# Attention scores with two heads per 32-row group of queries and keys, in a fused AdaLN block and rotation

## The chip, the cores and the metric

One core of a Trainium2 chip runs one program. The metric is device time in microseconds, the median of several executions. A core has five engines with queues of their own: TensorE (PE, with its weight loads PEld), VectorE (DVE), ScalarE (ACT), GpSimd (POOL) and SyncE (SP), which issues the DMAs here. They meet at semaphores only. Matmuls write PSUM, eight banks of 512 f32 columns on 128 partitions.

## The reference

Everything is f32. B = 16 sequences, L = 128 tokens, C = 144 channels, H = 16 heads of D = 9.

```python
ada = silu(c) @ W_ada + b_ada
shift_msa, scale_msa, gate_msa, shift_mlp, scale_mlp, gate_mlp = split(ada, 6)
h = modulate(layernorm(x), shift_msa, scale_msa)
q, k, v = heads(h @ W_qkv + b_qkv)
attn = softmax((q * D ** -0.5) @ k.T)               # per sequence and head, 128 x 128
x = x + gate_msa * ((attn @ v) @ W_proj + b_proj)
h = modulate(layernorm(x), shift_mlp, scale_mlp)
x = x + gate_mlp * (gelu(h @ W_fc1 + b_fc1) @ W_fc2 + b_fc2)
U, _ = qr(P)                                        # P is 144 x 64
R = expm(A)                                         # A skew, 64 x 64, one for each sequence, from silu(cond) @ W.T + b
x = x + (((x @ U) @ R) - x @ U) @ U.T
```

## The kernel before

The program has three parts: a start (loads, adaLN's modulations, first transposes), an attention loop over the sequences written out as attention(b) for b = 0 to 17, and a tail (MLP and rotation in quads of four sequences). The loop takes from about 28 to 255 us of the span. Three jobs are woven into it by hand:

- **Attention.** attention(b) scores sequence b, weighs sequence b-1 and closes sequence b-2; it also prepares q, k and v of b+1.
- **The QR of P.** 63 elimination steps, each a row pair made by TensorE (step_rows, L1435 to 1445) and then eleven small VectorE instructions (eliminations, L885 to 916) with a little work on GpSimd. A step's rows need the step before. Up to four steps (q = 0 to 3) go into one attention(b); where b % 5 is 4 there are three.
- **The matrix exponential** (generator_stage, L1257): entries in b = 0 and 1, transposes in 5, norms in 6, powers in 7 to 9, two products in 10, one in 11, squarings of two products each in 12 to 15. Its products use banks 4 and 5, which the transposes of keys and queries use too.

TensorE's order in one attention(b) is (L1479 to 1530): scores(b, 0); step 0; values(b-2, 1); qkv(b+1); scores_T(b-1, 0); heads_back and step 1; keys_T(b+1) and queries_T(b+1); scores(b, 1); values(b-1, 0); the generator's products; step 2; normalized_T(b-2); scores_T(b-1, 1); step 3; projection(b-2); queries_again_T(b); inputs_T(b+2). VectorE's is: maximum(b, 0), elimination 0; elimination 1, statistics, divided(b-2); maximum(b, 1), elimination 2, normalized(b+2); elimination 3, gated(b-2), with the generator's arithmetic between (L973 to 1049).

How a sequence's scores come about: ScalarE copies q (scaled) and k from PSUM into the stacks qstk and kstk, in which a head has SL = 32 columns: nine for its dimensions, one that is 1 in the keys and takes the negated maximum in the queries, and zeros. Four heads fill 128 columns, so stack_T (L1333) makes four transposes of 128 columns into one bank: head 4j + r lies on rows 32r to 32r + 31 of tile j. ScalarE copies the bank to KT (keys_copied, L522), QT (queries_copied, L527) and, after the maxima are in, again to QM (queries_again, L533).

scores(b, g) multiplies QT and KT for eight heads, each a matmul over 32 rows with 128 columns, row group r into bank r (L1363 to 1367). maximum(b, g) on VectorE takes the row maxima of the four half banks (L969). queries_again_T transposes the stack with the maxima in it, and scores_T(b, g) multiplies KT and QM into the transposed scores less their maxima (L1375 to 1379). ScalarE's exponentials write E (L551), and values (L1394) multiplies E with V. Scores, transposed scores and their readers share banks 0 to 3.

An f32 matmul shows as two records in the trace, an f32 transpose as one.

In what order ScalarE works around this in attention(b): queries_again(b-1), modulated(b+1), the copy of the weighed heads, stacked(b+1), exponentials(b-1, 0), keys_copied(b+1), queries_copied(b+1), the generator's evacuations, oT, exponentials(b-1, 1) (L553 to 585). queries_copied(b+1) waits for scores(b, 1), since there is one QT.

Of the kernel before, what the change touches and what calls it, by code (L numbers as in the profile page):

```python
# [6 lines left out]
ALU = mybir.AluOpType  # L7
# [58 lines left out]
def adaln_block_then_rotation(nc, x, cond, W_qkv, b_qkv, W_proj, b_proj, W_fc1, b_fc1, W_fc2, b_fc2,  # L66
# [11 lines left out]
    SL = 32  # L78
# [14 lines left out]
    with ExitStack() as ctx:  # L93
# [3 lines left out]
        def sem(name):  # L97
# [48 lines left out]
        QT, QM = sb("QT", [128, 4, 128]), sb("QM", [128, 4, 128])  # L146
        KT = [sb(f"KT{p}", [128, 4, 128]) for p in range(3)]
# [72 lines left out]
        (s_xn, s_xnT, s_hT, s_qkv, s_stk, s_V, s_kT, s_KT, s_qT, s_QT, s_S, s_max, s_qmT, s_qz, s_QM, s_ST, s_E, s_pv, s_O, s_Ot,  # L220
         s_on, s_OnT, s_oT, s_proj, s_pr, s_x1, s_st1) = (
            sem(n) for n in ("s_xn", "s_xnT", "s_hT", "s_qkv", "s_stk", "s_V", "s_kT", "s_KT", "s_qT", "s_QT", "s_S", "s_max",
# [255 lines left out]
        def _(act):  # L478
# [40 lines left out]
            def keys_copied(b):  # L519
                act.wait_ge(s_kT, b + 1)  # L520
                wait(act, s_ST, 2 * b - 4)
                nc.scalar.activation(KT[b % 3][:, :, :].rearrange("p j t -> p (j t)"), bank[5], ACT.Copy).then_inc(s_KT, 1)  # L522

            def queries_copied(b):
                act.wait_ge(s_qT, b + 1)
                wait(act, s_S, 2 * b)
                nc.scalar.activation(QT[:, :, :].rearrange("p j t -> p (j t)"), bank[4], ACT.Copy).then_inc(s_QT, 1)  # L527

            def queries_again(b):
# [3 lines left out]
                nc.scalar.activation(QM[:, :, :].rearrange("p j t -> p (j t)"), bank[5], ACT.Copy).then_inc(s_QM, 1)  # L533
# [60 lines left out]
            stacked(0)  # L594
            keys_copied(0)
# [38 lines left out]
        def _(dve):  # L634
# [38 lines left out]
            def gram_copied():  # L673
# [6 lines left out]
                nc.vector.tensor_copy(PT[:, :], bank[7][0:RD, 2 * RD:2 * RD + C]).then_inc(s_Z, 1)  # L680

# [284 lines left out]
            def maximum(b, g):  # L966
                dve.wait_ge(s_S, 2 * b + g + 1)
                wait(dve, s_qmT, b - 1)
                nc.vector.tensor_reduce(qstk[b % 2][:, 8 * g:8 * g + 8, D:D + 1].rearrange("p (j r) a -> p r (j a)", r=4),  # L969
                                        scored(g).rearrange("p r (j m) -> p r j m", j=2),  # L970
# [81 lines left out]
            modulations(0, bank[6])  # L1052
            gram_copied()
# [73 lines left out]
        def _(pe):  # L1127
# [205 lines left out]
            def stack_T(dst, stack, done):  # L1333
                for j in range(4):
                    ins = pe.transpose(dst[:, 128 * j:128 * j + 128], stack[:, 4 * j:4 * j + 4, :].rearrange("p h s -> p (h s)"),  # L1335
                                       ident[:, :])
# [18 lines left out]
            def scores(b, g):  # L1355
# [7 lines left out]
                for j in range(2):  # L1363
                    for r in range(4):
                        rows = slice(32 * r, 32 * r + 32)
                        ins = mm(bank[r][:, 128 * j:128 * j + 128], QT[rows, 2 * g + j, :], KT[b % 3][rows, 2 * g + j, :],  # L1366
# [331 lines left out]
```

## Time and profile before

| | |
|---|---|
| median of 3 runs | 321.51 us |
| lowest, highest | 319.87, 322.42 us |
| the profiled execution | span 323.8 us; no other time of it is recorded |
| mean granted TensorE clock | 0.935 of 2.4 GHz |
| busy | PE 282.6, DVE 212.7, ACT 130.7, POOL 105.0 us |

A page of the profile gives busy times, the span in slices, the chain of work that ended last, and groups of instructions by line, with the mean duration of one and the idle time before them. Records of TensorE overlap: the mean of one is longer than the step from one to the next, and the chain's pieces show the step. A granted clock of 1.00 is 2.4 GHz, of 0.50 1.2 GHz. TensorE's clock stands at half in five stretches of this execution, in all about 41 us.

### The profile page before, as it was taken

The page shows a single profiled execution, that of the slowest core. Times are in us where ns is not written, and L with a number is a line of the kernel's source. Part 1 is how long each engine was busy: PE and PEld are TensorE (multiplying, and loading weights), DVE is VectorE, ACT ScalarE, POOL GpSimd, SP SyncE. Part 2 cuts the span into 40 slices and gives each one's busy share as a digit, 9 for nine tenths or more (in the row PEclk, how much of TensorE's full clock was granted, in tenths as well). Part 3 has the DMA queues.
Part 4 walks back from the last instruction along what each step waited for, and adds up shares of the span by engine and source line. Part 5 has one row for each costly group of instructions (what it writes and reads, how often), then busy time and mean ns, then how long its engine had stood idle before and what let it go on. Part 6 is the DMA issues. An engine that isn't in the chain of part 4 may idle for free.

```text
span 323.8 us, 8835 instructions
## 1 busy us (share of the span) xinstructions
PE 282.6 (87%) x3215; PEld 204.5 (63%) x3215; DVE 212.7 (66%) x948; ACT 130.7 (40%) x274; POOL 105.0 (32%) x298
## 2 busy tenths in 40 slices
PE   2898889879899998888998889989987489999995
PEld 2765355566666766647777567677775344756983
DVE  6147654785777998748997697757575665733543
ACT  1023323442555445416554444555444316340321
POOL 7413141524233324224442234323234088500000
PEclk9998967985999999959999999999999769999999
DMA  7936000000000000000000000000000000000013
GB/s 200 241 98 257 3 10 0 11 9 10 1 3 2 2 3 2 2 0 4 3 2 2 3 2 2 1 4 3 2 2 1 2 0 2 4 0 0 2 38 109
DMA packets 9779, 8.44 MB, mean 26 GB/s; under 512 B 2064, under 2 KB 9334, under 8 KB 9608
## 3 DMA queue, kind: packets, MB, share of 16 engines
q1 hardware_dynamic: 9380, 7.11, 7.7%
q10 hardware_dynamic: 356, 0.75, 0.8%
q8 instruction: 27, 0.44, 0.6%
q14 instruction: 16, 0.13, 0.1%
HBM read 6.40 MB, written 1.20 MB: 23 GB/s over the span
## 4 chain that ended last, share of the span: by engine, by line
PE 70%; DVE 20%; issue 6%; ACT 2%; POOL 1%; ACTq 1%; DVEq 0%
PE banks L1330 6%; PE banks L1440 6%; PE banks L1366 5%; PE banks L1598 5%; PE banks L1335 5%; PE banks L1331 5%; PE banks L1582 4%; PE banks L1198 4%; PE banks L1378 4%; PE banks L1444 3%; PE banks L1394 3%; DVE qstk L969 2%; DVE cB L914 2%; PE banks L1415 2%; PE banks L1404 2%
## 5 line engine op out<-in xcount | busy, mean ns | idle before, releaser
L412 POOL TENSOR_TENSOR root<-rec,mhalf 128x1 f32<-128x1 f32 x63 | 34.5, 548 | 151.0 <-DVE Z L910 151.0
L969 DVE TENSOR_REDUCE qstk<-banks 128x8 f32<-128x1024 f32 x32 | 39.0, 1219 | 7.9 <-PE banks L1366 6.3
L895 DVE RECIPROCAL rec<-banks 128x1 f32<-128x1 f32 x63 | 10.3, 164 | 46.0 <-PE banks L1444 43.0
L551 ACT ACTIVATE E<-banks 128x1024 f32<-128x1024 f32 x32 | 32.8, 1026 | 9.0 <-PE banks L1378 8.8
L1440 PE MATMUL banks<-Z,ident 128*128 128x65 f32 x126 | 26.6, 295 | 9.2 <-DVE Z L916 8.7
L1440 PEld LDWEIGHTS banks<-Z,ident 128*128 128x128 f32 x126 | 20.3, 201 | 18.5 <-issue 12.0
L1378 PEld LDWEIGHTS banks<-QM,KT 32*128 32x128 f32 x512 | 18.0, 193 | 16.5 <-issue 16.4
L1378 PE MATMUL banks<-QM,KT 32*128 32x128 f32 x512 | 24.2, 305 | 2.4 <-issue 2.4
L1366 PE MATMUL banks<-KT,QT 32*128 32x128 f32 x512 | 24.8, 310 | 1.7 <-DVE wskT L714 1.6
L1444 PE MATMUL banks<-Z,ident 128*128 128x64 f32 (+62 forms) x126 | 24.0, 272 | 0.4 <-DVE Z L916 0.4
L1366 PEld LDWEIGHTS banks<-KT,QT 32*128 32x128 f32 x512 | 18.4, 197 | 8.3 <-issue 8.3
L1394 PE MATMUL banks<-E,V 128*32 128x128 f32 x512 | 21.9, 292 | 1.4 <-ACT E L551 0.7
L1444 PEld LDWEIGHTS banks<-Z,ident 128*128 128x128 f32 x126 | 20.3, 202 | 0.6 <-issue 0.6
L1335 PE MATMUL banks<-ident,qstk 128*128 128x128 f32 x128 | 20.1, 282 | 0.0
L1330 PE MATMUL banks<-wqkv,hT 128*128 128x432 f32 x32 | 19.9, 709 | 0.0
L1598 PE MATMUL banks<-wfc2a,gT 128*128 128x144 f32 x128 | 18.6, 288 | 0.0
L1598 PEld LDWEIGHTS banks<-wfc2a,gT 128*128 128x128 f32 x128 | 16.7, 190 | 2.3 <-issue 2.3
L543 ACT ACTIVATE qstk<-banks 128x144 f32<-128x144 f32 x16 | 4.9, 309 | 32.2 <-PE banks L1331 32.2
L910 DVE SCALAR_TENSOR_TENSOR Z<-banks,cG,Z 128x64 f32<-128x64 f32 x63 | 17.8, 282 | 0.0
L509 ACT ACTIVATE hT<-banks,mod 128x128 f32<-128x128 f32 (+1 forms) x32 | 12.5, 445 | 12.9 <-PE banks L1317 12.9
L1331 PE MATMUL banks<-wqkv,hT 128*128 128x432 f32 x32 | 17.5, 633 | 0.0
L916 DVE SCALAR_TENSOR_TENSOR Z<-banks,cB,Z 128x63 f32<-128x63 f32 (+62 forms) x63 | 15.8, 251 | 2.2
(249 smaller groups left out, 627.2 us busy)
## 6 DMA issues: line engine op xcount, KB each, us to landing
gates<-gates_dram SPq DMA_DIRECT2D x1, 2304.0 KB, 9.7
x_all<-in_x_dram SPq DMA_DIRECT2D x4, 288.0 KB, 6.1
out_dram<-x_all SPq DMA_DIRECT2D x8, 144.0 KB, 2.0
wskew<-in_L_cond_W_dram SPq DMA_DIRECT2D x4, 283.5 KB
A<-v SPq DMA_DIRECT2D x63, 4.0 KB
wada<-in_L_cond_W_ada_dram ACTq DMA_DIRECT2D x1, 432.0 KB
wfc1a<-in_L_cond_W_fc_dram SPq DMA_DIRECT2D x1, 288.0 KB
wfc2a<-in_L_cond_W_fc_dram SPq DMA_DIRECT2D x1, 288.0 KB
```

What stands on the lines that cost most here:

```text
L412: link(nc.gpsimd.tensor_tensor(root[:, at], rec[:, at], mhalf[:, 0:1], ALU.pow))
L551: nc.scalar.activation(E[:, g, :, :, :].rearrange("p r j t -> p r (j t)"), scored(g), ACT.Exp).then_inc(s_E, 1)
L969: nc.vector.tensor_reduce(qstk[b % 2][:, 8 * g:8 * g + 8, D:D + 1].rearrange("p (j r) a -> p r (j a)", r=4), scored(g).rearrange("p r (j m ...
L1330: mm(bank[4][:, 0:3 * C], hT1[:, :], wqkv1[:, :], start=True, stop=False)
L1331: mm(bank[4][:, 0:3 * C], hT2[:, :], wqkv2[:, :], start=False, stop=True).then_inc(s_qkv, 1)
L1335: ins = pe.transpose(dst[:, 128 * j:128 * j + 128], stack[:, 4 * j:4 * j + 4, :].rearrange("p h s -> p (h s)"), ident[:, :])
L1366: ins = mm(bank[r][:, 128 * j:128 * j + 128], QT[rows, 2 * g + j, :], KT[b % 3][rows, 2 * g + j, :], start=True, stop=True)
L1378: ins = mm(bank[r][:, 128 * j:128 * j + 128], KT[b % 3][rows, 2 * g + j, :], QM[rows, 2 * g + j, :], start=True, stop=True)
L1394: ins = mm(bank[6][own, cols], weights[:, first:first + 32], E[:, g, 2 * (i % 2) + p, i // 2, :], start=(p == 0), stop=(p == 1))
L1440: mm(bank[7][:, cols], ident[:, k:k + 1].to_broadcast([128, 128]), Z[:, cols], start=True, stop=True).then_inc(s_Grow, 1)
L1444: mm(bank[7][:, cols], ident[:, k - 1:k].to_broadcast([128, 128]), Z[:, cols], start=True, stop=True).then_inc(s_Brow, 1)
L1598: mm(dst, gT[Q % 2][:, k, cols], wfc2a[:, k, :], start=(k == 0), stop=False)
```

## The change

A head gets SL = 16 columns of the stacks, so eight heads fill 128 columns and a stack takes two transposes. Heads 8g + 2r and 8g + 2r + 1 share row group r of tile g. The queries QT and QM hold both heads' rows. The keys are copied twice into KX, each time with the rows of the other head multiplied by zero: the scale is a column of `side`, which is 1 on the rows of one head of each pair. The first scores stream both masked copies, 256 columns, past one stationary block of queries; the transposed scores take each masked copy as the stationary block and stream the queries, 128 columns, as before. side is made on VectorE in the start by two reduces of the identity.

```diff
-    SL = 32
+    SL = 16
...
-        QT, QM = sb("QT", [128, 4, 128]), sb("QM", [128, 4, 128])
-        KT = [sb(f"KT{p}", [128, 4, 128]) for p in range(3)]
+        QT, QM = sb("QT", [128, 2, 128]), sb("QM", [128, 2, 128])
+        KX = [sb(f"KX{p}", [128, 2, 2, 128]) for p in range(3)]
+        side4, side = sb("side4", [128, 2, 4]), sb("side", [128, 2])
...
             def keys_copied(b):
                 act.wait_ge(s_kT, b + 1)
                 wait(act, s_ST, 2 * b - 4)
-                nc.scalar.activation(KT[b % 3][:, :, :].rearrange("p j t -> p (j t)"), bank[5], ACT.Copy).then_inc(s_KT, 1)
+                for p in range(2):
+                    ins = nc.scalar.activation(KX[b % 3][:, :, p, :], bank[5][:, 0:256].rearrange("p (j t) -> p j t", j=2),
+                                               ACT.Identity, scale=side[:, p:p + 1])
+                ins.then_inc(s_KT, 1)
...
-                nc.scalar.activation(QT[:, :, :].rearrange("p j t -> p (j t)"), bank[4], ACT.Copy).then_inc(s_QT, 1)
+                nc.scalar.activation(QT[:, :, :].rearrange("p j t -> p (j t)"), bank[4][:, 0:256], ACT.Copy).then_inc(s_QT, 1)
...
-                nc.scalar.activation(QM[:, :, :].rearrange("p j t -> p (j t)"), bank[5], ACT.Copy).then_inc(s_QM, 1)
+                nc.scalar.activation(QM[:, :, :].rearrange("p j t -> p (j t)"), bank[5][:, 0:256], ACT.Copy).then_inc(s_QM, 1)
...
             stacked(0)
+            act.wait_ge(s_side, 1)
             keys_copied(0)
...
+            def sides():
+
+                dve.wait_ge(k_id, N_ID)
+                link(nc.vector.tensor_reduce(side4[:, :, :], ident[:, :].rearrange("p (r a s) -> p a r s", a=2, s=SL), AX.X, ALU.add))
+                nc.vector.tensor_reduce(side[:, :], side4[:, :, :], AX.X, ALU.add).then_inc(s_side, 1)
...
-                nc.vector.tensor_reduce(qstk[b % 2][:, 8 * g:8 * g + 8, D:D + 1].rearrange("p (j r) a -> p r (j a)", r=4),
-                                        scored(g).rearrange("p r (j m) -> p r j m", j=2),
+                nc.vector.tensor_reduce(qstk[b % 2][:, 8 * g:8 * g + 8, D:D + 1].rearrange("p (r q) a -> p r (q a)", r=4),
+                                        scored(g).rearrange("p r (q m) -> p r q m", q=2),
...
             moments(0)
             modulations(0, bank[6])
+            sides()
             gram_copied()
...
             def stack_T(dst, stack, done):
-                for j in range(4):
-                    ins = pe.transpose(dst[:, 128 * j:128 * j + 128], stack[:, 4 * j:4 * j + 4, :].rearrange("p h s -> p (h s)"),
+                for j in range(2):
+                    ins = pe.transpose(dst[:, 128 * j:128 * j + 128], stack[:, 8 * j:8 * j + 8, :].rearrange("p h s -> p (h s)"),
                                        ident[:, :])
...
-                for j in range(2):
-                    for r in range(4):
-                        rows = slice(32 * r, 32 * r + 32)
-                        ins = mm(bank[r][:, 128 * j:128 * j + 128], QT[rows, 2 * g + j, :], KT[b % 3][rows, 2 * g + j, :],
-                                 start=True, stop=True)
+                for r in range(4):
+                    rows = slice(32 * r, 32 * r + 32)
+                    ins = mm(bank[r][:, 0:256], QT[rows, g, :], KX[b % 3][rows, g, :, :].rearrange("p q m -> p (q m)"),
+                             start=True, stop=True)
                 ins.then_inc(s_S, 1)
...
-                for j in range(2):
+                for p in range(2):
                     for r in range(4):
                         rows = slice(32 * r, 32 * r + 32)
-                        ins = mm(bank[r][:, 128 * j:128 * j + 128], KT[b % 3][rows, 2 * g + j, :], QM[rows, 2 * g + j, :],
-                                 start=True, stop=True)
+                        ins = mm(bank[r][:, 128 * p:128 * p + 128], KX[b % 3][rows, g, p, :], QM[rows, g, :], start=True, stop=True)
                 ins.then_inc(s_ST, 1)
...
-                        ins = mm(bank[6][own, cols], weights[:, first:first + 32], E[:, g, 2 * (i % 2) + p, i // 2, :],
+                        ins = mm(bank[6][own, cols], weights[:, first:first + 32], E[:, g, i, p, :],
                                  start=(p == 0), stop=(p == 1))
```

## Rows read from the trace of the kernel before

**Rows 1.** The page, part 4: shares of the chain by engine

```profile
PE 70%; DVE 20%; issue 6%; ACT 2%; POOL 1%; ACTq 1%; DVEq 0%
```

**Rows 2.** The chain in block 13: start us, length us, what

```profile
211.76 0.92 PE banks L1335 x8
...
213.47 0.61 ACT QT L527
214.21 2.08 PE banks L1198 x64
...
216.88 0.17 DVE rec L895
```

**Rows 3.** The timeline in block 13, values and the second maximum

```profile
213.28 0.64 PE L1394 MATMUL banks<-E,V 128*32 128x128 f32 x16
...
213.94 1.22 DVE L969 TENSOR_REDUCE qstk<-banks 128x8 f32<-128x1024 f32 x1
```

**Rows 4.** The chain in block 3, after step 1

```profile
84.77 0.64 DVE qstk L969
```

**Rows 5.** The chain after blocks 2, 3 and 7, at half and at full clock

```profile
73.91 0.85 PE banks L1335 x4
...
81.81 0.37 PE banks L1404 x2
...
88.75 0.44 PE banks L1335 x4
89.40 0.66 PE banks L1366 x16
...
93.51 0.37 PE banks L1404 x2
...
139.23 1.17 PE banks L1366 x16
...
146.24 0.37 PE banks L1404 x2
```

**Rows 6.** Groups by line: busy us, mean ns of one, idle before

```profile
L969 DVE TENSOR_REDUCE qstk<-banks 128x8 f32<-128x1024 f32 x32 | 39.0, 1219 | 7.9 <-PE banks L1366 6.3 <-issue 1.4
L1366 PE MATMUL banks<-KT,QT 32*128 32x128 f32 x512 | 24.8, 310 | 1.7 <-DVE wskT L714 1.6
L1394 PE MATMUL banks<-E,V 128*32 128x128 f32 x512 | 21.9, 292 | 1.4 <-ACT E L551 0.7 <-DVE tmp L922 0.7
L1335 PE MATMUL banks<-ident,qstk 128*128 128x128 f32 x128 | 20.1, 282 | 0.0
```

**Rows 7.** The chain in the start and in block 1: transposes of keys and queries

```profile
20.95 1.02 PE banks L1335 x8
...
49.53 1.72 PE banks L1335 x8
```

**Rows 8.** Groups of ScalarE by line

```profile
L522 ACT ACTIVATE KT<-banks 128x512 f32<-128x512 f32 x16 | 9.6, 598 | 4.8 <-PE banks L1335 3.0
L509 ACT ACTIVATE hT<-banks,mod 128x128 f32<-128x128 f32 x16 | 7.3, 454 | 12.9 <-PE banks L1317 12.9
L561 ACT ACTIVATE Osb<-banks 128x256 f32<-128x256 f32 x16 | 6.2, 385 | 16.9 <-PE banks L1394 16.9
L582 ACT ACTIVATE oT<-banks 128x128 f32<-128x128 f32 x16 | 4.4, 278 | 16.8 <-PE banks L1411 16.5
```

**Rows 9.** The group of a small reduce on VectorE

```profile
L752 DVE TENSOR_REDUCE nsc<-over 128x8 f32<-128x96 f32 x1 | 0.3, 252 | 0.0
```

**Rows 10.** Windows: length, busy (x instructions) of PE, PEld, DVE, ACT, POOL, PEclk, DMA

```profile
68.00:70.00 2.00, 0.73 (x6) 0.44 (x6) 1.97 (x9) 0.42 (x2) 0.00 (x0) 1.00 0.03 7
70.00:72.00 2.00, 1.45 (x18) 1.21 (x18) 1.88 (x12) 0.49 (x1) 0.86 (x3) 0.59 0.04 10
...
178.00:180.00 2.00, 0.94 (x8) 0.70 (x7) 1.93 (x11) 0.62 (x2) 0.97 (x4) 1.00 0.02 4
180.00:182.00 2.00, 1.62 (x26) 1.28 (x30) 0.77 (x2) 0.80 (x2) 0.36 (x1) 1.00 0.00 0
```

More of the change, by code:

```diff
@@ L218, in adaln_block_then_rotation @@
             sem(n) for n in ("s_Gp", "s_Z", "s_var1", "s_rstd1", "s_var2", "s_rstd2"))
-        (s_xn, s_xnT, s_hT, s_qkv, s_stk, s_V, s_kT, s_KT, s_qT, s_QT, s_S, s_max, s_qmT, s_qz, s_QM, s_ST, s_E, s_pv, s_O, s_Ot,
+        (s_xn, s_xnT, s_hT, s_qkv, s_stk, s_V, s_kT, s_KT, s_qT, s_QT, s_side, s_S, s_max, s_qmT, s_qz, s_QM, s_ST, s_E, s_pv, s_O, s_Ot,
          s_on, s_OnT, s_oT, s_proj, s_pr, s_x1, s_st1) = (
-            sem(n) for n in ("s_xn", "s_xnT", "s_hT", "s_qkv", "s_stk", "s_V", "s_kT", "s_KT", "s_qT", "s_QT", "s_S", "s_max",
+            sem(n) for n in ("s_xn", "s_xnT", "s_hT", "s_qkv", "s_stk", "s_V", "s_kT", "s_KT", "s_qT", "s_QT", "s_side", "s_S", "s_max",
                              "s_qmT", "s_qz", "s_QM", "s_ST", "s_E", "s_pv", "s_O", "s_Ot", "s_on", "s_OnT", "s_oT", "s_proj",
```

## The prediction

> **What bounds the kernel now.** I read the chain of work that ended last first. It is TensorE for 70% of the span and VectorE for 20% [rows 1]. The share alone says little, so I read the chain piece by piece and sorted the sixteen blocks b = 0 to 15 by what releases elimination step (b, 2).
>
> In block 13 TensorE is never idle between step (13, 1) and step (13, 2). The chain runs through the eight transposes of keys and queries (0.92 us), the first scores, the copy of the queries on ScalarE (0.61) and the 64 products of a squaring (2.08); VectorE gets the new rows only at 216.88 [rows 2]. The copy stands in the chain because the products write bank 4 and wait for s_QT: values(12, 0) end at 213.92 [rows 3], the products start at 214.21, and the 0.25 us or so between is a stall.
>
> In block 3 there is no product. There VectorE is late: after step (3, 1) it eliminates, divides and takes the maximum, and that maximum is the chain at 84.77 [rows 4]. TensorE waits meanwhile. Work taken from TensorE in that place buys nothing.
>
> Between step (b, 3) and step (b+1, 1) it is the other way round in most blocks: projection, queries_again_T, inputs_T, scores, values and qkv follow each other without a gap, and VectorE's maximum and elimination (b+1, 0) end 0.2 to 0.6 us before heads_back asks for them.
>
> **The change part by part.**
>
> *Transposes.* keys_T, queries_T and queries_again_T go from four to two 128-column transposes. Four are 0.44 us of chain at 88.75 [rows 5], 0.11 each; their mean duration of 282 ns [rows 6] overlaps and isn't the price. So a pair of stacks saves 0.46 and queries_again_T 0.22 at full clock, twice that at half clock.
> - Stacks, where TensorE is late: the start 1.02 to 0.51; block 0 the same, 0.5; block 1, at half clock, 1.72 to 0.86 (the first and the last of the three stand in [rows 7]): 1.9 us together. Blocks 7, 10, 12, 13, 14 save 0.46 each: 2.3. In block 9 scores_T(8, 1) waits for the maximum, which leaves 0.25. Blocks 2 to 6, 8 and 11 save nothing: VectorE is late there, with moments, triangles, matrix work or the maximum alone. Sum 4.45.
> - queries_again_T: ten transitions lie on an unbroken TensorE chain, after blocks 2, 3, 4, 5, 6, 8, 9, 11, 12, 13. Block 2's runs at half clock, 0.85 at 73.91 [rows 5], and gives 0.43. After 4 and 9 there is no step 3 and the bank is read by the exponentials until just before, after 5 VectorE comes level: I take 0.45 for these three and 0.22 for the other six. Sum 2.2. Blocks 0 and 1 (VectorE), 7 (the flag, below), 10 (halves_joined on bank 4) and 14 (exponentials) give nothing.
>
> *The stall for queries_copied.* Its copy goes from 512 to 256 columns. A plain ScalarE copy of 512 takes 598 ns, of 256 385 [rows 8]: 0.21 less. Ahead of it keys_copied becomes two copies of 256 with a scale read from a tile. No row has that form. Nearest: with two pointer operands a 128x128 copy takes 454 (L509; its row of 445 mixes in the second, 16x128 copy), without 278 [rows 8], so about 88 a pointer: 385 + 88 = 473 each, and since two copies overlap by about 0.11, 0.83 for both against 0.60. Bounds: 0.66 (pointer free) and 1.0 (the whole 176 for one). The keys are transposed 0.23 earlier, so the two copies end at step rows + 1.2, and the queries, which must also wait for scores(b, 1) at + 1.2, at + 1.6; TensorE ends values(b-1, 0) at + 1.7. The stall is gone in blocks 7, 10, 12, 13, 14 [rows 2, 3]: 5 x 0.25 = 1.25. With 1.0 for the pair 0.1 of it stays. By the Trainium skill, ScalarE: Activation LUTs, section What ACT_TABLE_LOAD costs, a pointer operand adds about 93 ns and back-to-back copies overlap by as much: 0.86 for the pair, the same answer here.
>
> *First scores.* Eight matmuls (16 records) of 128 columns become four (8 records) of 256; the columns streamed stay 1,024. 16 records take 0.66 us of chain at 89.40 [rows 5], 41 ns each, though one lasts 310 [rows 6]: four row groups run at once. With 0.11 us for 128 columns, as the transposes have it, streaming alone is 4 x 0.11 = 0.44 before and 2 x 0.22 = 0.44 after. The rest is weight loads and latency: I take no change; bounds -0.09 (busy 21.9 us for the 32 groups of values, which load 32 columns, against 24.8) and, with the same size the other way, +0.1 [rows 6]. Some 20 of the 32 groups are on the chain: -1.8 to +2. The transposed scores, maximum, exponentials and values keep instruction count and shapes; only heads move to other places.
>
> *sides().* Two small reduces on VectorE and one link. 128x8 from 96 elements takes 252 ns [rows 9], the maximum's 1,024 take 1,219 [rows 6], 1.04 ns an element more; so 128 take 0.28 and eight at most 0.17 us. They stand where VectorE would wait for TensorE's first Gram matrix; behind them are Z's copies and normalized(0). All of it is hidden; without that cover it costs 0.45 once. keys_copied(0) asks for s_side only after the first keys are transposed, at 21 us. The memsets of the stacks halve on an idle GpSimd. No DMA is added or moved.
>
> Sum: 4.45 + 2.2 + 1.25 = 7.9 us. 323.8 - 7.9 = 315.9 for the profiled span. That span lies 2.3 above the median of the runs, so in runs 321.5 - 7.9 = 313.6.
>
> **What it gives back: the clock.** TensorE gets its work off the path too. In blocks 2 to 6, 8 and 11 it now reaches the same VectorE wait 0.46 us earlier and idles longer. The granted clock fell from 2.4 to 1.2 GHz after such a pause: TensorE 0.73 us busy in 68 to 70, the clock 0.59 in 70 to 72. After a pause of 0.94 at 178 to 180 it stayed at 1.00 [rows 10]. So a pause makes a fall possible, not certain, and the milder pauses of blocks 3, 6, 8, 11 and 15 now deepen towards those. The price: from queries_again_T to the end of heads_back 8.27 us at half clock (73.91 to 82.18) against 5.13 (88.75 to 93.88), 3.1 more; in the later fall, scores(8, 0) to heads_back, 7.38 (139.23 to 146.61) against 4.48 (89.40 to 93.88), 2.9 more [rows 5]; the step and projection ahead are slowed also. I take 3.5 for one fall. By the Trainium skill, TensorE: Matmul & The Clock Gate, section HAM oscillation, idle gaps between matmuls put the engine back to half rate until it has been busy again; the trace agrees at five places, and this is a rule against taking filler off TensorE.
>
> **The rivals.**
> 1. *One more fall than before* (likeliest): 313.6 + 3.5 = 317.1. For it: five blocks with a deeper pause. Chance 0.35.
> 2. *No more falls*: 313.6. For it: 178 to 180 kept the clock [rows 10]; the existing falls get cheaper as less work is slowed. Chance 0.30.
> 3. *Two or three more falls*: 320.6 to 324.1; the gain is gone. Against it: a slowed block fills its own next pause. Chance 0.20.
> 4. *VectorE takes over.* Its maxima are 39.0 us [rows 6] and it is the chain in seven blocks already. If it also becomes late in blocks 7 and 9 to 14, the stack gain and the stall (2.55 + 1.25) go: 317.4. Against it: in block 13 its maximum ends at 215.16 and it waits until 216.88, 1.7 us [rows 2, 3]. Chance 0.08.
> 5. *Slower: wide matmuls of the row groups run one after the other.* Eight records of 0.22 are 1.7 us or more instead of 0.66, some 20 times on the chain: +21, 335. It decides (over 1% slower) from 0.55 us more a group, 1.2 us in all. Against it: the 128-column records overlap four ways from the same row groups. Chance 0.04.
> 6. *The change does nothing* because the transposes' places are filled by waits: about 321. Chance 0.03.
>
> **How the numbers follow.** About 1%, 3.2 us, is what a measurement can tell here. I predict 317.0, case 1. The range takes in case 2 with cheaper scores (312.0) and the nearer end of case 3 (321.5), leaving out 0.2. Below 318.3 lie case 2, most of 1 and 4: 0.60. Within 1%: the rest of 1 and 4, two falls, case 6: 0.30. Slower: three or more falls and case 5: 0.10.
>
> **What would show it.** the stack transposes' pieces at x4 (stacks) and x2 in the chain, 0.46 and 0.22; no ScalarE copy of queries in the chain of blocks 12 to 14 and that distance from step 1 to the products 0.7 shorter; the keys' copy x32 at about 470 ns; the first scores x8 in a chain piece of about 0.66 us; maxima still 1,219 ns; TensorE's busy time some 10 us less (96 x 0.11); the low-clock stretches, five before, counted and placed. Wrong would be: a first-score group over 0.9 us at full clock, ScalarE in the chain ahead of the scores, or no additional fall with a time above 317, which would mean that my list of blocks where TensorE is late is too long.

## The result: 334.5 us against 320.7, slower

| | before | after |
|---|---|---|
| median | 320.69 us (4 runs, 318.85 to 322.42) | 334.47 us (4 runs, 334.02 to 336.94) |
| ratio | | 1.0441 (95%: 1.037 to 1.0512) |
| profiled execution | span 323.8 us | 334.02 us, span 332.2 us |
| mean granted clock | 0.935 | 0.884 |
| half clock, in all | 41.2 us, 5 stretches | 77.0 us, 12 stretches |

The change was predicted at 317.0 us, in a range from 312.0 to 321.5. It is 4.4% slower. Ratios here and below leave out single runs with an unusually low clock, so they can stand a little off the ratio of the medians.

The medians are 13.8 us apart, the profiled spans only 8.4. A run's time is 1.8 us above its span (334.02 and 332.2), so the profiled execution of before was some 5 us longer than the median one. In the comparisons below, executions of before that took 319 to 321.5 us have mean granted clocks of 0.955 to 0.967, against 0.935 in the profile. What is read from the pair of profiles therefore understates what the change costs in most executions.

The page of the profile after: the span, busy times, the granted clock in 40 slices, the shares of the chain, and the groups of the maxima and the first scores.

```profile
span 332.2 us, 8150 instructions
PE 288.4 (87%) x2863; PEld 195.2 (59%) x2863; DVE 212.7 (64%) x950; ACT 127.4 (38%) x290; POOL 104.4 (31%) x298
PEclk9998969676799797959899585999999769999998
PE 73%; DVE 18%; issue 5%; ACT 2%; POOL 1%; ACTq 0%; DVEq 0%
L980 DVE TENSOR_REDUCE qstk<-banks 128x8 f32<-128x1024 f32 x32 | 39.0, 1218 | 12.3 <-PE banks L1377 10.4
L1377 PE MATMUL banks<-KX,QT 32*128 32x256 f32 x256 | 27.6, 505 | 2.5 <-DVE wskT L725 1.6
```

TensorE has 352 records fewer (2,863 against 3,215: 96 transposes, and 256 because the first scores come in half as many) and is busy 5.8 us longer (288.4 against 282.6). That points at its clock. With the clock at or near full in both (the last two runs below) the same 352 records fewer make TensorE's busy time shorter, 278.4 us against 290.9. The clock line of before, for comparison:

```profile
PEclk9998967985999999959999999999999769999999
```

Read in narrow windows, the clock stands at half from (us, length):

| before | after |
|---|---|
| 29.4 (3.4), 43.1 (10.2), 70.4 (10.2), 138.6 (6.8), 254.7 (10.2) | 29.9 (3.4), 40.2 (6.8), 57.2 (6.8), 70.9 (10.2), 87.9 (3.4), 111.8 (3.4), 125.5 (3.4), 142.6 (6.8), 156.2 (3.4), 183.5 (6.8), 197.2 (10.2), 262.0 (10.2) |

The stretches of before add up to 41.0 us and those of after to 75.1. The rest of the totals, 0.2 and 1.9 us, lies at the very end of the span, where TensorE has no work left; totals of other kernels below can hold as much.

Yet where the clock is full, the chain after looks as the change meant it to. The chain of block 13 after (start us, length us, what), to be read against [rows 2]:

```profile
221.63 0.49 PE banks L1347 x4
222.12 0.03 issue
222.15 0.71 PE banks L1377 x8
222.86 0.57 PE banks L1404 x16
223.44 0.07 issue
223.51 2.08 PE banks L1210 x64
...
226.17 0.17 DVE rec L906
```

The stacks' transposes take 0.49 instead of 0.92, ScalarE's copy of the queries is gone from the chain, and the stall ahead of the generator's products is 0.07. The first scores take 0.71. In the same place in before, behind the stacks of block 13, their 128-column form took 0.70, so the form changes next to nothing:

```profile
212.69 0.70 PE banks L1366 x16
```

**Two accounts.** The last instruction of each elimination (L916 before, L927 after) occurs once a step, and the width of its operand, 64 less the step's number, tells which step it is. The distance from step (b, 0) to step (b+1, 0) is the length of block b. For block 13, the timeline of before, then of after (start us, length us, instruction):

```profile
210.09 0.23 DVE L916 SCALAR_TENSOR_TENSOR Z<-banks,cB,Z 128x11 f32<-128x11 f32 x1
...
223.48 0.23 DVE L916 SCALAR_TENSOR_TENSOR Z<-banks,cB,Z 128x7 f32<-128x7 f32 x1
```

```profile
219.90 0.23 DVE L927 SCALAR_TENSOR_TENSOR Z<-banks,cB,Z 128x11 f32<-128x11 f32 x1
...
232.54 0.23 DVE L927 SCALAR_TENSOR_TENSOR Z<-banks,cB,Z 128x7 f32<-128x7 f32 x1
```

13.39 against 12.64: 0.75 us saved, at full clock in both. Two kernels told of below (the last two runs) do the same work with the clock at full through all of these blocks. With them the loop, from the first elimination to the last, splits into its two causes:

| us | before | after | difference |
|---|---|---|---|
| loop at full clock | 206.4 | 201.9 | -4.5 |
| added by half clock | 12.8 | 25.9 | +13.1 |
| loop as profiled | 219.2 | 227.8 | +8.6 |

The spans differ by 332.2 - 323.8 = 8.4. So in this pair of profiles the whole loss lies in the loop and is the clock's: the change saves 4.5 us of work and pays 13.1 for it. For the medians, 13.8 us apart, the clock's part would have to be about 18 us, an estimate: 13.8 + 4.5. Block by block, what the change saves where the clock is full in both, beside what was predicted:

| block | 0 | 1 | 2 | 3 | 4 | 5 | 6 | 7 | 8 | 9 | 10 | 11 | 12 | 13 | 14 | 15 |
|---|---|---|---|---|---|---|---|---|---|---|---|---|---|---|---|---|
| measured | 0.29 | 0.16 | 0 | 0.16 | -0.12 | 0 | 0.08 | 0.73 | 0.13 | 0.13 | 0.63 | 0.05 | 0.93 | 0.75 | 0.53 | 0 |
| predicted | 0.50 | 0.86 | 0.43 | 0.22 | 0.15 | 0.15 | 0.22 | 0.71 | 0.22 | 0.40 | 0.71 | 0.22 | 0.93 | 0.93 | 0.71 | 0 |

### The profile page after: what moved, and what is told of

It reads as the page before. It is cut to its first block, busy times and chain, and to the rows that moved or that the text cites. A ratio compares the mean times of both kernels' runs of the same rounds, so it can differ in the third digit from the quotient of the medians.

```text
span 332.2 us, 8150 instructions
## 1 busy us (share of the span) xinstructions
PE 288.4 (87%) x2863; PEld 195.2 (59%) x2863; DVE 212.7 (64%) x950; ACT 127.4 (38%) x290; POOL 104.4 (31%) x298
## 4 chain that ended last, share of the span: by engine, by line
PE 73%; DVE 18%; issue 5%; ACT 2%; POOL 1%; ACTq 0%; DVEq 0%
PE banks L1377 6%; PE banks L1342 6%; PE banks L1450 6%; PE banks L1343 5%; PE banks L1608 5%; PE banks L1404 5%; PE banks L1389 4%; PE banks L1210 4%; PE banks L1592 4%; PE banks L1454 4%; PE banks L1347 3%; PE banks L1425 2%; PE banks L1414 2%; DVE cB L925 2%; PE banks L1426 1%
## 5 line engine op out<-in xcount | busy, mean ns | idle before, releaser
L980 DVE TENSOR_REDUCE qstk<-banks 128x8 f32<-128x1024 f32 x32 | 39.0, 1218 | 12.3 <-PE banks L1377 10.4
L1450 PE MATMUL banks<-Z,ident 128*128 128x65 f32 x126 | 28.4, 311 | 10.0 <-DVE Z L927 8.2
L1450 PEld LDWEIGHTS banks<-Z,ident 128*128 128x128 f32 x126 | 21.6, 214 | 25.8 <-issue 17.4
L1377 PE MATMUL banks<-KX,QT 32*128 32x256 f32 x256 | 27.6, 505 | 2.5 <-DVE wskT L725 1.6
L1389 PEld LDWEIGHTS banks<-QM,KX 32*128 32x128 f32 x512 | 18.5, 197 | 18.5 <-issue 18.5
L1389 PE MATMUL banks<-QM,KX 32*128 32x128 f32 x512 | 24.7, 309 | 2.6 <-issue 2.4
L1454 PE MATMUL banks<-Z,ident 128*128 128x64 f32 (+62 forms) x126 | 25.1, 281 | 0.4 <-DVE Z L927 0.4
L1404 PE MATMUL banks<-E,V 128*32 128x128 f32 x512 | 22.8, 301 | 1.7 <-DVE tmp L933 0.9
L1454 PEld LDWEIGHTS banks<-Z,ident 128*128 128x128 f32 x126 | 21.5, 214 | 0.6 <-issue 0.6
L1342 PE MATMUL banks<-wqkv,hT 128*128 128x432 f32 x32 | 21.8, 771 | 0.0
L1343 PE MATMUL banks<-wqkv,hT 128*128 128x432 f32 x32 | 19.8, 712 | 0.0
L1377 PEld LDWEIGHTS banks<-KX,QT 32*128 32x128 f32 x256 | 12.2, 216 | 10.8 <-issue 10.8
L1404 PEld LDWEIGHTS banks<-E,V 128*32 128x32 f32 x512 | 13.2, 117 | 7.9 <-issue 6.1
L927 DVE SCALAR_TENSOR_TENSOR Z<-banks,cB,Z 128x63 f32<-128x63 f32 (+62 forms) x63 | 15.8, 251 | 2.2
```

Source lines behind the costliest of these rows:

```text
L1342: mm(bank[4][:, 0:3 * C], hT1[:, :], wqkv1[:, :], start=True, stop=False)
L1343: mm(bank[4][:, 0:3 * C], hT2[:, :], wqkv2[:, :], start=False, stop=True).then_inc(s_qkv, 1)
L1377: ins = mm(bank[r][:, 0:256], QT[rows, g, :], KX[b % 3][rows, g, :, :].rearrange("p q m -> p (q m)"), start=True, stop=True)
L1389: ins = mm(bank[r][:, 128 * p:128 * p + 128], KX[b % 3][rows, g, p, :], QM[rows, g, :], start=True, stop=True)
L1404: ins = mm(bank[6][own, cols], weights[:, first:first + 32], E[:, g, i, p, :], start=(p == 0), stop=(p == 1))
L1450: mm(bank[7][:, cols], ident[:, k:k + 1].to_broadcast([128, 128]), Z[:, cols], start=True, stop=True).then_inc(s_Grow, 1)
```

## The experiments

The question was why the clock falls so much more often. Two theories stood against each other at first: TensorE lacks the 96 transposes, whatever else the change does; or the new form of the first scores, 256 columns and a masked second copy, does it. A third was that nothing but chance differs between executions. Except where something else is said, each edit is to the changed kernel.

### The transposes put back

```diff
             def stack_T(dst, stack, done):
-                for j in range(2):
+                for j in (0, 1, 0, 1):
```

> The changed kernel with each stack transpose made twice (the same two tiles again), so that TensorE streams as many transposes as in the kernel before; everything else as changed. Theory A, that the time was lost because the missing transposes let the granted clock fall more often (12 falls and 77.0 us at half clock after, 5 and 41.2 before): the falls go back to 5 or 6, about 40 us at half clock, and the time to that of the kernel before, 318 to 322 us. Theory B, that the 256-column scores or the masked keys lower the clock or cost time by themselves: the falls stay at 10 or more and the time rises by the added transposes to about 340 us.

Measured: 320.29 us (10 runs, 318.97 to 329.99), ratio to before 0.9902 (0.9854 to 0.995), as theory A had it. The profiled run has a clock of 0.957 and 27.3 us at half clock:

```profile
PEclk9999899979999989869999999999999669999999
```

Doing as many transposes as before, half of them to no use at all, takes 12 to 14 us off the changed kernel (332.8 and 334.5 us in its two measurements). Everything else of the change is still in, and does no harm. Block 13 takes 13.14 us here, 0.25 less than before: that is the stall for the queries' copy, alone.

### The first scores in 128 columns

```diff
-                for r in range(4):
-                    rows = slice(32 * r, 32 * r + 32)
-                    ins = mm(bank[r][:, 0:256], QT[rows, g, :], KX[b % 3][rows, g, :, :].rearrange("p q m -> p (q m)"),
-                             start=True, stop=True)
+                for p in range(2):
+                    for r in range(4):
+                        rows = slice(32 * r, 32 * r + 32)
+                        ins = mm(bank[r][:, 128 * p:128 * p + 128], QT[rows, g, :], KX[b % 3][rows, g, p, :],
+                                 start=True, stop=True)
```

> The changed kernel with the first scores in 128 columns again, one matmul for each of the two masked copies (16 records a group instead of 8). Theory A (missing transposes): no change in falls or time, 332 to 337 us. Theory B (the wide matmuls, half as many records, count for less in what keeps the clock up): the half-clock time drops from 77 to about 45 us and the time to 314 to 320 us.

Measured: 332.83 us (328.24 to 334.03), ratio 1.0206 (1.0064 to 1.0349); 68.6 us at half clock in 11 stretches.

```profile
PEclk9999958585899897969799699999979859999999
```

Ten falls in the loop and one in the tail are still there, so the form of the first scores is not what brings them. The ratio is a little below that of the changed kernel (1.044, and 1.043 when run again), and a small part of the loss may be the form's; the runs don't settle it. For the work the form hardly matters: block 13 takes 12.66 us in this form and 12.64 with 256 columns. The chain of this kernel in block 12 shows the first scores behind the stacks at 0.73 with 128 columns, so the 0.71 of after is not the wide form's doing:

```profile
206.43 0.48 PE banks L1347 x4
206.92 0.03 issue
206.95 0.73 PE banks L1378 x16
```

### The transposes taken out of the kernel before

Edit to the kernel before. Heads 8 to 15 are left out: only two tiles are transposed, and ScalarE reads them twice to fill its 512 columns (the copies to QT and QM likewise).

```diff
-                nc.scalar.activation(KT[b % 3][:, :, :].rearrange("p j t -> p (j t)"), bank[5], ACT.Copy).then_inc(s_KT, 1)
+                nc.scalar.activation(KT[b % 3][:, :, :].rearrange("p (a j) t -> p a (j t)", a=2), bank[5][:, 0:256].rearrange("p (a n) -> p a n", a=1).to_broadcast([128, 2, 256]), ACT.Copy).then_inc(s_KT, 1)
...
             def stack_T(dst, stack, done):
-                for j in range(4):
+                for j in range(2):
```

> The kernel before with two transposes a stack instead of four; ScalarE still copies 512 columns, reading the two transposed tiles twice, so heads 8 to 15 get the rows of heads 0 to 7 and their attention is left out. All matmuls and copies keep their sizes. Theory A: the half-clock time rises to 65 to 80 us with it and the time comes to 330 to 336 us. Theory B: the half-clock time stays at about 41 us and the time falls by the 6.65 us that the prediction gave to the transposes, to 313 to 315 us.

Measured: 332.39 us (326.04 to 333.79; three of the four runs lie above 331), clock 0.886 to 0.926; 75.3 us at half clock in the profile.

```profile
PEclk9999969867679995969999699999997559999999
```

With the old layout, the old scores and copies of the old size, taking out the transposes alone brings the falls and a loss of the same kind, though block 13 gets shorter here too (12.85 us against 13.39). Putting as many back into the changed kernel takes the loss away, with all the rest of the change in place. Together the two show the cause: the missing transposes.

### Filler in the waits

Matmuls whose result nobody reads go where TensorE waits anyway: about step 2, behind normalized_T, ahead of step 3, ahead of inputs_T in blocks 7 and 10, and at four places of the last attention(b) and the tail (5 or 6 each), 110 matmuls in all.

```diff
+            def fill(n, to=6):
+                for _ in range(n):
+                    mm(bank[to][:, 400:512], ident[:, :], ident[:, 0:112], start=True, stop=True)
...
+                fill({2: 2, 3: 3, 4: 3}.get(b, 0))
                 step(b, 2)
+                fill({5: 3, 6: 3, 11: 6}.get(b, 0))
...
+                fill({2: 7, 4: 1}.get(b, 0))
...
+                fill({0: 8, 1: 5, 2: 4, 3: 4, 6: 4, 8: 4}.get(b, 2 if (b, 3) in STEPS else 0))
                 step(b, 3, projection if closing(b) else None)
...
+                if b in (7, 10):
+                    pe.wait_ge(s_E, 2 * b)
+                    fill(8, 3)
```

> The changed kernel with idle filler: 112-column f32 matmuls of the identity, about 0.19 us each at full clock, into bank columns that nobody reads, only at the places where TensorE waits (2 to 4 ahead of each step 3, 2 or 3 ahead of step 2 in blocks 2 to 4 and behind it in blocks 5, 6 and 11, 7 or 8 ahead of the waits of blocks 0, 1, 2, 7 and 10, and at the end of the loop). Theory A: the clock falls at most 3 times, under 20 us at half clock, and the time comes to 300 to 312 us. Theory B, that the time went into something other than the clock: the time stays at 330 us or more.

Measured: 308.24 us (308.08 to 310.85), ratio to before 0.9557 (0.9462 to 0.9653); clock 0.994 to 1.0, one fall of 3.5 us left.

```profile
span 306.5 us, 8590 instructions
PE 281.8 (92%) x3083; PEld 202.3 (66%) x3083; DVE 212.6 (69%) x950; ACT 126.4 (41%) x290; POOL 104.0 (34%) x298
PEclk9999899999999999999999999999999999999999
```

The changed kernel with 220 more TensorE records is 24 to 26 us faster than without them. A price of half clock follows: 334.02 - 308.35 = 25.7 us for 77.0 - 3.5 = 73.5 us less of it, 0.35 us for each. Within the loop it is a little more: 25.9 us for 64.9 in after and 12.8 for 30.7 in before, 0.40 and 0.42.

### The changed kernel once more

No edit.

> The changed kernel once more, beside the next three on one chip. If the clock explains the loss, its runs scatter with their mean granted clock: 330 to 337 us at a clock of 0.88 to 0.90, and 12 falls or so again.

Measured: 332.75 us (329.25 to 335.86), ratio 1.0427 (1.0327 to 1.0526). The profile has 8 stretches and 68.8 us:

```profile
PEclk9998999969899958789997867999996559999999
```

The result stands. The stretches are fewer than in the first profile (the table behind the experiments has the blocks), and the kernel before too ranges from 319 us at a clock of 0.962 to 330 at 0.926 from one execution to the next. So which pause ends in a fall is fixed in part only.

### The same filler in the kernel before

The edit is the diff above, made to the kernel before at the same places.

> The kernel before with the same filler matmuls at the same places. With the clock up in both, the difference to the changed kernel with filler (308.2 us) is what the change is worth at full clock. If the prediction's sum of 7.9 us is right (less what falls at half clock, about 7.2): 315 to 317 us. If the change is worth nothing or costs something at full clock: 308 us or less.

Measured: 315.97 us (314.89 to 317.49), ratio 0.9859 (0.9804 to 0.9914), clock 0.995. Filler alone is worth 1.4% to the old kernel, and the change under filler another 315.97 - 308.24 = 7.7 us. That looks like the predicted 7.9 and isn't quite it. The profiled pair is 9.2 us apart (spans 315.7 and 306.5). 3.1 us of that lie ahead of the first elimination (its last instruction begins at 27.6 us and 24.5). Kernels whose starts are the same scatter by as much there: 24.5 and 27.1 in the changed kernel with the fuller filler and with the lighter one below. About 1.3 is what the fuller filler costs the kernel before more than it costs the changed one (block 11 takes 13.11 us with it and 12.79 with the lighter one).

### Only the keys' and queries' transposes twice

```diff
-                stack_T(bank[5], kstk, s_kT)
+                stack_T(bank[5], kstk, s_kT, (0, 1, 0, 1))
...
-                stack_T(bank[4], qstk[b % 2], s_qT)
+                stack_T(bank[4], qstk[b % 2], s_qT, (0, 1, 0, 1))
```

> The changed kernel with only the transposes of keys and queries made twice; those of the queries with their maxima once. The missing stack transposes stand just ahead of VectorE's pauses, the others well ahead of the next one. If the pauses of the late blocks decide, the falls of blocks 3, 5, 6, 8 and 11 go away and the time is 316 to 322 us, as with all of them twice. If only the amount of TensorE work counts, two thirds of the effect: 322 to 327 us.

Measured: 326.24 us (323.52 to 329.68), ratio 1.0227 (1.0128 to 1.0325); 44.5 us at half clock in the profile. The falls of blocks 3, 5, 6, 8 and 11 are gone, as the first expectation had it, but the time is that of the second: block 10 still falls, and the tail has a stretch of 20.5 us.

```profile
PEclk9999899978999999779998799999995569999999
```

### Only queries_again_T twice

The same edit at queries_again_T alone: `stack_T(bank[5], qstk[b % 2], s_qmT, (0, 1, 0, 1))`.

> The changed kernel with only the transposes of the queries with their maxima made twice, 0.22 us a block. They stand on the path in most blocks and a third of the removed work is in them. If the clock follows what is removed ahead of the pauses at step 2, the falls stay near 10 and the time is 330 to 336 us. If every bit of work counts: 325 to 330 us.

Measured: 322.82 us (10 runs, 318.17 to 330.77), ratio 0.9915 (0.9848 to 0.9982); 44.6 us at half clock in the profile.

```profile
PEclk9999967985899997998899999999999569999999
```

I had expected 330 to 336 here, from the theory that the missing work matters only where it stands ahead of the pauses about step 2. In that form the theory fell: queries_again_T is a third of what was removed, stands elsewhere, and wins back more than the other two thirds do (ratios 0.9915 and 1.0227).

The kernels with part of the work put back also split the saving at full clock. Block 13 takes 12.64 us with the change, 12.99 with the stacks' transposes twice, 12.79 with queries_again_T twice, 13.14 with both, 13.39 before. The stacks are 0.35, queries_again_T 0.15, the stall 0.25, and the sum is the 0.75 found above. In block 12 the five lengths are 12.46, 12.80, 12.82, 13.14 and 13.39: stacks 0.34, queries_again_T 0.36, stall 0.25 (0.02 of them overlap).

### Less filler

The places of the first filler with about 60% of its matmuls.

```diff
-                fill({2: 2, 3: 3, 4: 3}.get(b, 0))
+                fill({2: 1, 3: 2, 4: 2}.get(b, 0))
                 step(b, 2)
-                fill({5: 3, 6: 3, 11: 6}.get(b, 0))
+                fill({5: 2, 6: 2, 11: 4}.get(b, 0))
...
-                fill({0: 8, 1: 5, 2: 4, 3: 4, 6: 4, 8: 4}.get(b, 2 if (b, 3) in STEPS else 0))
+                fill({0: 6, 1: 3, 2: 2, 3: 2, 6: 2, 8: 2}.get(b, 1 if (b, 3) in STEPS else 0))
```

> The changed kernel with about 60% of the filler. In the chain of the fuller version the filler itself ended some pauses late (1.07 us of it ahead of step 3 in block 3). If the clock needs little: still fewer than 3 falls and 304 to 308 us. If the pauses come back: 2 to 4 more falls than with the full filler and 310 to 320 us.

Measured: 310.42 us (308.32 to 311.4), ratio 0.9681 (0.9604 to 0.9757), clock 0.987 to 0.994. The blocks are as long as with the full filler, to 0.1 us, and the one fall left stands at the start (32.6 to 36.0). I had expected 304 to 308 us with so few falls; in this profile the first elimination comes 2.6 us later than with the full filler. The fuller filler isn't needed for the clock.

### Filler at the pauses about step 2 only

Three filler matmuls about step 2 in blocks 2 to 6, 8 and 11 and none elsewhere.

```diff
+                fill({2: 3, 3: 3, 4: 3}.get(b, 0))
                 step(b, 2)
+                fill({5: 3, 6: 3, 8: 3, 11: 3}.get(b, 0))
```

> The changed kernel with filler only in the seven blocks where the prediction had VectorE late (2 to 6, 8, 11): three matmuls, 0.56 us, in the wait at step 2, in place of the 0.46 us of transposes that the change took out ahead of it. If the extra falls come from that place alone: falls back to 5 or 6, 30 to 45 us at half clock, and, since the work now lies in the wait and not on the path, 312 to 317 us. If the other transposes and blocks matter as much: 318 to 328 us.

Measured: 319.54 us (315.97 to 324.43), clocks 0.924 to 0.950; 31.8 us at half clock in the profile. That is 13 to 15 us less than the changed kernel, for seven times three matmuls, and between the two expectations. The falls in blocks 3, 5, 6, 8 and 11 are gone; those at the start, in 2, 7, 10 and the tail are left. Blocks 0 and 1 have none either, though nothing is filled there; the changed kernel's second profile has none there too.

```profile
PEclk9998899977999999989998799999999579999999
```

### Less filler, and some at the start

The lighter filler, and seven matmuls ahead of the first scores.

```diff
             def attention(b):
+                if b == 0:
+                    fill(7)
```

> The changed kernel with the lighter filler (310.4 us, one fall at 32.6 us left) and seven more matmuls of it ahead of the first scores, where TensorE waits 1.6 us. If the last fall goes: clock 1.00 in all runs and 305 to 309 us. If it stays, 308 to 311 us.

Measured: 309.94 us (308.07 to 310.55), ratio 0.9608 (0.9525 to 0.9691). The clock is 1.00 in all four runs, and the time a little above the 305 to 309 us expected for that:

```profile
span 306.0 us, 8486 instructions
PEclk9999999999999999999999999999999999999999
```

This and the full filler, 308.2 and 309.9 us, both beat both kernels, by about 4% against before.

### The same in the kernel before

The edits of the run above, made to the kernel before.

> The kernel before with the lighter filler and the seven matmuls ahead of the first scores: the same filler as the changed kernel's last version (309.9 us, clock 1.00). Less filler can be late in fewer places. If the change is worth 7 to 8 us at full clock: 316 to 318 us at a clock of 0.99 to 1.00. If the fuller filler had cost the kernel before more than the changed one, 312 to 315 us, and the change is worth 3 to 5 us.

Measured: 314.15 us (5 runs, 312.99 to 319.47), ratio 0.9793 (0.97 to 0.9886), 4.2 us above its counterpart. Its profile has one fall, at 247.5 us, behind the last elimination.

```profile
span 315.1 us, 9171 instructions
```

The loop takes 206.6 us here and 201.9 in its counterpart. Of the 4.7 us between, 0.2 is this filler's own cost in block 14 (12.66 us against 12.42 in before as it was), so the change itself is worth 4.5 us, near the 4.2 between the medians. This is the answer that the expectation put at 3 to 5 us. The table above has these two kernels' blocks, with block 14 taken from before.

### In which blocks the clock falls

One profile each, a stretch put down to the block in which it begins:

| kernel | blocks | tail | half clock, us |
|---|---|---|---|
| before | start, 0, 2, 7 | yes | 41.2 |
| both transposes twice | start, 2, 6, 7 | yes | 27.3 |
| stacks' transposes twice | start, 2, 7, 10 | yes | 44.5 |
| queries_again_T twice | 0, 2, 3, 6, 8 | yes | 44.6 |
| filler about step 2 only | start, 2, 7, 10 | yes | 31.8 |
| after | start, 0, 1, 2, 3, 5, 6, 7, 8, 10, 11 | yes | 77.0 |
| after, again | start, 2, 3, 6, 7, 10, 11 | yes | 68.8 |
| 128-column scores | 0, 1, 2, 3, 5, 6, 7, 8, 10, 15 | yes | 68.6 |
| before, less transposes | 0, 1, 2, 3, 6, 7, 10 | yes | 75.3 |

Blocks 3, 6, 8 and 11 fall in the four rows at the bottom, not each in each. In the two kernels in which the stacks' transposes alone come back, or filler takes their place about step 2, none of them falls; with both transposes back, block 6 does. Block 10 goes on falling in those two and stops only with queries_again_T. So the place of the work does matter, block by block, and there are two places. With one profile for a kernel, and falls that come and go between executions, this is a pattern that the profiles suggest and not more.

## Where the prediction held and where it failed

**Number of further falls: the step that failed.** Prediction: one more fall likeliest (0.35), two or three at 0.20, and with three or more the only way to a loss beside case 5. Measured: seven more, in blocks 1, 3, 5, 6, 8, 10 and 11. The mechanism, deeper pauses of TensorE that bring further falls, was right, and four of the five blocks that the prediction named (3, 6, 8, 11 and 15) are among them. What failed is that I named five candidates and counted one. With the saving as measured (4.5 us) and one fall at the predicted price the sum would have been 321.5 - 4.5 + 3.5 = 320.5, inside the range; with seven falls at that price and all else as predicted it would have been 321.5 - 7.9 + 24.5 = 338.1, outside. [Rows 10] had a pause that ended in a fall and one, 178 to 180, that did not, and I took the second as evidence for safety. The windows of after (TensorE's busy time is the first number behind the length; the granted clock is the last but two) show that such a row doesn't sort them:

```profile
124.00:126.00 2.00, 1.17 (x15) 1.05 (x8) 1.40 (x10) 1.02 (x1) 0.91 (x3) 0.87 0.00 0
126.00:128.00 2.00, 2.00 (x11) 1.54 (x14) 1.72 (x10) 0.82 (x3) 1.31 (x4) 0.50 0.00 0
...
154.00:156.00 2.00, 1.16 (x21) 0.89 (x19) 1.93 (x12) 1.40 (x3) 0.89 (x3) 1.00 0.00 0
156.00:158.00 2.00, 2.00 (x11) 1.74 (x10) 1.93 (x11) 0.19 (x2) 1.01 (x2) 0.55 0.04 8
```

TensorE is busy for 1.16 or 1.17 us of two and the clock falls; it is busy for 0.94 at 178 to 180 in before [rows 10] and the clock stays. Read in hindsight, five falls in a kernel whose sixteen blocks repeat much the same pauses were a sign that many places could fall together once TensorE's work was thinned, not one; that is my reading, and no run here forecasts a fall from a pause. Rival 3's "a slowed block fills its own next pause" did not hold either: in after, stretches begin at 57.2, 70.9 and 87.9 us, in three blocks one behind the other. The Trainium skill's rule on idle gaps (TensorE: Matmul & The Clock Gate, section HAM oscillation) pointed the right way, that idle time of TensorE brings half clock. In size the traces differ: the page's gaps are waits for DMA, longer than any pause of TensorE in these two loops, where the longest is 1.73 us, and some falls of after follow pauses of 0.7 to 0.8. The measurement decides: here many short pauses were enough.

Blocks 1, 5 and 10 were not on the list. It was made of places where the stacks' transposes end at a VectorE wait; that queries_again_T's missing 0.22 could do the same in block 10 was not asked.

**Price of a fall.** Predicted 3.5. Measured in the loop: 12.8 us for the 4 falls of before and 25.9 for the first 11 of after, 3.2 and 2.4 each. The seven more cost 13.1 together, 1.9 each, so for what the change adds the price was nearly twice too high; four of the seven new stretches last only 3.4 us.

**The sum at full clock.** Predicted 7.9, measured 4.5:

- The stall: 0.25 a block predicted, 0.25 measured. The pair of keys' copies, which the prediction put at 0.83 us, takes 0.84 in block 13.
- The stacks: 0.46 a block predicted, 0.35 measured. The chain's piece of transposes shrank by 0.43, but that piece isn't the price: from the first transpose's start to the first scores' start it is 1.00 us with eight transposes and 0.67 with four, in block 13 and its neighbours, and the first scores behind them last as long in both, to 0.02. With the stall, the five blocks 7, 10, 12, 13 and 14 (without queries_again_T's share) come to 3.1 against 3.55. Blocks 0 and 1 gave 0.45 together where 1.36 was put; 0.43 of what is missing was put there for block 1's half clock, which isn't a saving of work. For the start (0.51) the profiles resolve nothing: the first elimination's last instruction begins at 24.7 us before and at 24.6 after, but in the kernel before with the fuller filler, whose start is the same, at 27.6.
- queries_again_T: 2.2 predicted, in ten transitions. In blocks 12 and 13 it gave 0.36 and 0.15, in all the others together, with block 9's quarter for the stacks, 0.42: 0.9 against 2.45. The list of places where TensorE is the late one was too long, which the prediction named as a way of being wrong.

The chain at the end of block 4 shows how, first in the kernel before with filler and start filler, then in the changed kernel with the same, both at full clock:

```profile
92.41 0.44 PE banks L1335 x4
92.85 0.19 PE banks L1316
93.04 0.11 PE banks L1317
93.15 0.66 PE banks L1366 x16
```

```profile
89.05 0.22 PE banks L1347 x2
89.27 0.12 issue
89.38 0.30 PE banks L1328
89.68 0.11 PE banks L1329
89.79 0.64 PE banks L1377 x8
```

From queries_again_T's beginning to the first scores it is 0.74 us in both (93.15 - 92.41, 89.79 - 89.05). The 0.22 saved comes back as a gap of 0.12 and a first transpose of 0.30 instead of 0.19: inputs_T waits for VectorE's normalized rows, whose instruction in the changed kernel ends at 89.24. In before it ends at 92.60, 0.25 us ahead of the transpose that needs it. In the prediction's words, projection to qkv "follow each other without a gap". That was true of before, but another engine can be close behind a chain without a gap.

**What came out as said.** The keys' copies last 471 ns each (473 predicted), and the plain 256-column copies 384:

```profile
L524 ACT ACTIVATE KX<-banks,side 128x256 f32<-128x256 f32 x32 | 13.4, 471 | 2.0 <-PE banks L1347 2.0
L531 ACT ACTIVATE QT<-banks 128x256 f32<-128x256 f32 x16 | 6.2, 384 | 3.0 <-PE banks L1377 3.0
```

A pointer operand costs 87 ns by these two rows, whose function differs too (Identity and Copy); the Trainium skill, ScalarE: Activation LUTs, section What ACT_TABLE_LOAD costs, has about 93, and the trace agrees to 6 ns. The maxima stay at 1,218 ns, the first scores of all four row groups overlap (eight records in 0.64 to 0.71 us, rival 5 is out), and the two reduces of sides() are hidden. VectorE took over in some transitions (rival 4's mechanism), but blocks 7, 10, 12, 13 and 14, which that rival named, kept 0.53 to 0.93 us of their gain.

The prediction set the span of the profile against the median of the run times and found 2.3 us between them. Times run 1.8 us above spans, so the profiled execution was some 4 us longer than the median of then. This moves no term of the sum.

**What stays open.** Why 0.2 to 0.4 us of work a block, at either of two places, moves the clock so much, and why a given pause ends in a fall in one execution and not in the next. What in TensorE's activity decides, no run here tells.

## What to carry to other kernels

Before work is taken off TensorE, count the falls of the granted clock in the trace: a kernel that already has several, from pauses of one pattern, may get many more of them, and taking 0.7 us of work out of each block can cost more than it gives. What helped here was to fill the waits with matmuls that nobody reads, and to judge a change with the clock held: here the same change is +4.4% without filler and, with it, part of a kernel 4% faster than before. With the same filler in both, the change is worth 4.2 us in the medians, 1.3%; the filler alone takes 1.4 to 2.1% off the kernel before. And where one engine's chain runs without a gap, ask of each transition which other engine arrives with it; only the difference is saved.

## What the hardware showed that was not expected

- TensorE was busy for longer with less to do: 282.6 us for 3,215 records, 288.4 for 2,863, and 281.8 for 3,083 once filler kept the clock up.
- The falls followed pauses of TensorE of 0.7 to 1.7 us. In the loop of after, 12 of the 13 longest pauses (0.67 to 1.73 us) are followed by a fall within 4 us; of the 12 longest of before (0.68 to 1.73) only 4 are. In the changed kernel's second profile a pause of 1.74 us, at 38.4 us, has no fall behind it. So the length of a pause alone does not forecast a fall.
- The same program goes from 319 us at a mean clock of 0.962 to 330 at 0.926 between executions; with filler four runs lie within 308.1 and 310.9. Part of the scatter of this kernel was the clock's.
- Every stretch at half clock in the first profiles of both kernels lasts 3.4, 6.8 or 10.2 us. In the tail of other profiles, the changed kernel's second among them, there are stretches of 13.7 and 20.5 us.
